# A decoder layer on one core: one map of SBUF for all passes, loads of the next pass ahead of its start, and the first maxima inside the query projection

## What is computed

```python
# block 1, per token: the half of the 2752 gated values that is smallest is set to 0
s = silu(x @ w_gate.T); s[smallest 1376 of abs(s)] = 0
x = layernorm(x + (s * (x @ w_up.T)) @ w_down.T)
# block 2: 32 query heads on 8 key/value heads of 32 columns
q = x @ Wq; k = ctx @ Wk; v = ctx @ Wv
x = layernorm(x + softmax(q k^T / sqrt(32)) v @ Wo)
# block 3: w dequantised from 4 bits to bf16
x = layernorm(x + (bf16(x) @ w.T))
```

## Time and profile before

| what | value |
|---|---|
| median of 3 runs | 2564.99 us (2564.35 to 2570.72) |
| profiled execution: its time, its span | 2554.46 us, 2552.7 us |
| mean granted TensorE clock | 0.975 |
| busy: TensorE, its weight loads | 2402.1 us (94%), 2089.8 us (82%) |
| busy: VectorE, ScalarE, GpSimd | 1249.4 us (49%), 1047.4 us (41%), 1421.9 us (56%) |

### The profile page before, as it was taken

The page is one execution under the profiler, slowest core; times in us unless marked ns, Lnnn a source line. Parts: engine busy times, 40 slices in busy tenths (PEclk is TensorE's granted clock), DMA queues, the critical chain, the costliest instruction groups (busy, mean ns, idle before and its releaser), DMA issues. The chain is left out here.

```text
span 2552.7 us, 32567 instructions
## 1 busy us (share of the span) xinstructions
PE 2402.1 (94%) x12627; PEld 2089.8 (82%) x12640; DVE 1249.4 (49%) x1770; ACT 1047.4 (41%) x1531; POOL 1421.9 (56%) x635
## 2 busy tenths in 40 slices
PE   7999799999999999999999999999978989885998
PEld 6999689988899888999889998899946666654775
DVE  4762201872016930058500386345258888863665
ACT  2112133733337333354423463233337777780211
POOL 5344154775546855459554486444429998891221
PEclk9999889999999999999999999999969999997999
DMA  6555432233322333223333233579767776646773
GB/s 205 170 191 177 144 125 101 103 122 124 114 99 108 122 103 134 99 99 108 121 125 114 91 108 106 176 239 295 219 158 185 189 184 167 172 108 170 177 175 95
DMA packets 245995, 371.70 MB, mean 146 GB/s; under 512 B 124336, under 2 KB 176560, under 8 KB 245584
## 3 DMA queue, kind: packets, MB, share of 16 engines
q1 hardware_dynamic: 245840, 369.60, 47.8%
HBM read 290.15 MB, written 78.70 MB: 144 GB/s over the span
## 5 line engine op out<-in xcount | busy, mean ns | idle before, releaser
L823 POOL TENSOR_TENSOR gp_w_lo<-gp_raw,gp_w_hi 128x1024 fp32r<-128x1024 f32 (+2 forms) x300 | 723.1, 2412 | 603.9 <-ACT gp_w_hi L707 603.4
L58 PE MATMUL gp_acc<-gp_x_hi,gp_w_hi 128*128 128x448 f32 x1504 | 560.7, 373 | 26.5 <-POOL gp_w_lo L823 19.6
L59 PE MATMUL gp_acc<-gp_x_lo,gp_w_hi 128*128 128x448 f32 x1504 | 551.0, 366 | 0.0
L60 PE MATMUL gp_acc<-gp_x_hi,gp_w_lo 128*128 128x448 f32 x1504 | 550.5, 366 | 0.0
L707 ACT CAST gp_w_hi<-gp_raw 128x1024 fp32r<-128x1024 f32 (+2 forms) x300 | 307.0, 1026 | 301.7 <-PE gp_acc L60 300.8
L1251 POOL TENSOR_TENSOR ap_e_lo<-ap_e,ap_e_hi 125x1344 fp32r<-125x1344 f32 x112 | 341.8, 3081 | 70.1 <-DVE ap_e_hi L1328 45.6
L58 PEld LDWEIGHTS gp_acc<-gp_x_hi,gp_w_hi 128*128 128x128 f32 x1504 | 283.8, 189 | 50.4 <-issue 19.7
L60 PEld LDWEIGHTS gp_acc<-gp_x_hi,gp_w_lo 128*128 128x128 f32 x1504 | 283.7, 189 | 23.1
L59 PEld LDWEIGHTS gp_acc<-gp_x_lo,gp_w_hi 128*128 128x128 f32 x1504 | 284.1, 189 | 20.8
L339 DVE TENSOR_REDUCE gp_sel_unit<-gp_keys 112x4 f32<-112x2048 f32 x4 | 9.2, 2289 | 567.0 <-ACT gp_keys L720 567.0
L58 PE MATMUL gp_acc<-gp_h_hi,gp_w_hi 128*128 128x448 f32 (+1 forms) x704 | 266.4, 378 | 7.8 <-DVE gp_h_lo L885 5.0
(11 more groups left out here) (163 smaller groups left out, 4288.7 us busy)
## 6 DMA issues: line engine op xcount, KB each, us to landing
gp_raw<-in_w_gu SPq DMA_DIRECT2D x172, 512.0 KB, 3.2
gp_raw<-in_w_d SPq DMA_DIRECT2D x80, 512.0 KB, 3.4
cp_c_raw<-in_ctx_t SPq DMA_DIRECT2D x32, 750.0 KB, 6.3
gp_raw<-in_w_q SPq DMA_DIRECT2D x32, 512.0 KB, 3.8
q_scratch<-gp_q_out SPq DMA_DIRECT2D x64, 224.0 KB, 5.5
ap_qs<-q_scratch SPq DMA_DIRECT2D x32, 448.0 KB, 4.9
o_scratch<-ap_o_ab SPq DMA_DIRECT2D x64, 224.0 KB
ap_vs<-v_scratch SPq DMA_DIRECT2D x16, 773.4 KB
```

Of the source, the lines that this page charges most:

```text
L58: nc.tensor.matmul(out, wh, xh, start=first, stop=False)
L59: nc.tensor.matmul(out, wh, xl, start=False, stop=False)
L60: return nc.tensor.matmul(out, wl, xh, start=False, stop=last)
L823: last = nc.gpsimd.tensor_tensor(o, i, hi.bitcast(F32), ALU.subtract)
```

## The change

All tensors get their address by hand. `Bufs` takes a starting place for each pass and counts upwards; class `Carry` holds what two passes share: the buffers of x and of the gated weights, the query and key tiles, the first value tile, the sums, and the first two output tiles, with their semaphores. On this map:

- context_pass loads the first four gated weight tiles and half of x of the first group when it has three batches to go. It ends without waiting for its stores; ScalarE and VectorE wait for them in the next pass, before they first write where stored tensors lay (`await_context`).
- In gated_query_pass VectorE instead of GpSimd makes the low parts of the first group's x. The loads for batch 0 and the first of batch 1 are issued between the query stores, and the 16 pairs of batch 0 with their maxima are put behind projections 23 to 29, the turn behind 30. The stores of the last queries are awaited by SyncE and ScalarE inside the attention pass.
- In attend_pass half 0 of the queries and keys two batches ahead is fetched at h = 3 instead of h = 4, which puts it ahead of a `put_o`. In the last batch SyncE loads the first two output tiles; VectorE makes their quotients at positions 17 and 20; tile 0 is also split there. One memset of ones is left at the start.
- In finish_pass the last reciprocals are made and stored beside the first projection, and the stores of the last batches are awaited ahead of tile 8.

```diff
     def sb(self, name, shape, dt):
-        return self.ctx.enter_context(self.nc.sbuf_tensor(f"{self.tag}_{name}", shape, dt))
+        at = self.place
+        self.place += (math.prod(shape[1:]) * self.SIZES[dt] + 31) // 32 * 32
+        if self.place > self.ROOM:
+            raise ValueError(name)
+        return self.nc.alloc_sbuf_tensor_at(f"{self.tag}_{name}", shape, dt, offset=self.BASE + at)
...
+class Carry:
...
+    IDENT, LOW, XW, ACTS, KEYS, EARLY, MASK, SMALL = 0, 768, 24320, 77568, 116992, 120576, 161024, 208768
+    C_STORED = 162816
+    Q_OUT = 106240
+    QK1 = 153280
+    WO, PARTS, E, FIN = 768, 66304, 179648, 153280
...
+    XR, RAW, NQO, NO = 2, 4, 4, 3
+    PUT = 2 * 16
...
+        m = Bufs(nc, ctx, "cy", self.LOW)
+        self.x_raw = [m.sb(f"x_raw{i}", [P, 2, T], F32) for i in range(self.XR)]
+        self.raw = [m.sb(f"raw{i}", [P, KD * P], F32) for i in range(self.RAW)]
+        m.jump(self.EARLY)
+        self.qs, self.ks = [None, None], [None, None]
+        self.qs[0] = m.sb("qs0", [3 * HD + 2, 2, REP, 4, S], F32R)
+        self.ks[0] = m.sb("ks0", [3 * HD + 2, 2, 4, CP], F32R)
+        self.vs0 = m.sb("vs0", [KN, KT, KV, VW], F32R)
...
+    def fetch_qk(self, sp, qd, kd, n, half):
+
+        p, stack = n % 2, 3 * HD
+        q_rows = self.qs[p][:, half].bitcast(F32).rearrange("d j m q -> d (j m q)")
+        k_rows = self.ks[p][:, half].bitcast(F32).rearrange("d v c -> d (v c)")
+        for dst, src in ((q_rows[0:2 * HD], qd[n, half]), (k_rows[0:HD], kd[n, half, 0:HD]),
+                         (q_rows[2 * HD:stack], qd[n, half, 0:HD]), (k_rows[HD:stack], kd[n, half])):
+            sp.dma_start(dst, src).then_inc(self.qk_loaded[p][half], 16)
+
+    def put_max(self, sp, n):
+        p, stack = n % 2, 3 * HD
+        sp.wait_ge(self.nml, n + 1)
+        for row, src in ((stack, self.nm_hi), (stack + 1, self.nm_lo)):
...
+def load_tile(sp, od, rd, i, num, add, rec, loaded):
+    t = slice(i * P, (i + 1) * P)
+    for n in range(i * P // S, ((i + 1) * P - 1) // S + 1):
+        q0, q1 = max(i * P - n * S, 0), min((i + 1) * P - n * S, S)
+        at = slice(n * S + q0 - i * P, n * S + q1 - i * P)
+        for s, dst in enumerate((num, add)):
+            sp.dma_start(dst[:, :, at], od[n, :, s].rearrange("h d j q -> (d j) h q")[:, :, q0:q1]).then_inc(loaded, 16)
+    for j in range(REP):
+        sp.dma_start(rec[j:P:REP], rd.rearrange("h j t -> j h t")[j, :, t].unsqueeze(0).broadcast_to([HD, KV, P])
+                     ).then_inc(loaded, 16)
 
...
                     for h in range(2):
                         load(n + 2, h)
                 store(n)
+                if n == B - 3:
+                    for i in range(cy.RAW):
+                        sp.dma_start(cy.raw[i][:], w_gu[i]).then_inc(cy.raw_loaded[i], 16)
+                        if i < cy.XR:
+                            sp.dma_start(cy.x_raw[i][:], x_t[0, :, 2 * i:2 * i + 2]).then_inc(cy.x_loaded[i], 16)
             sp.wait_ge(copied, KD)
-            sp.dma_start(w3_dram, w_io[:]).then_inc(w3_stored, 16)
-            for s in stored:
-                sp.wait_ge(s, 48 * (B // 2))
-            sp.wait_ge(w3_stored, 16)
+            sp.dma_start(w3_dram, w_io[:]).then_inc(cy.w3_stored, 16)
...
+    PAIRS = {23: (0, 1), 24: (2, 3), 25: (4, 5), 26: (6, 7), 27: (8, 9), 28: (10, 11, 12), 29: (13, 14, 15)}
+    TURN_MAX = 30
...
-            for i in range(XC):
+            for i in range(XR, XC):
                 load_x(0, i)
-                load(i)
-            for n in range(XC, NALL + AHEAD + 4):
+            for n in range(RAW, NALL + AHEAD + 4):
...
+                if p == 20:
+                    cy.await_context(sp)
+                    for s in q_stored:
+                        sp.wait_ge(s, 32 * KD // NQO)
+                    cy.fetch_qk(sp, q_v, k_v, 0, 0)
+                if p == 23:
+                    cy.fetch_qk(sp, q_v, k_v, 0, 1)
+                if p == 26:
+                    sp.dma_start(cy.vs0[:].bitcast(F32).rearrange("p t v w -> p (t v w)"), vd[0]).then_inc(cy.v_loaded[0], 16)
+                if p == 28:
+                    for i in range(XS):
+                        sp.wait_ge(y1_stored[i], 16 * len(range(i, B, XS)))
+                    sp.wait_ge(back, 2 * B)
+                    cy.fetch_qk(sp, q_v, k_v, 1, 0)
+                if p == 32:
+                    cy.put_max(sp, 0)
...
             for i in range(XC):
-                x_split_hi(0, i)
                 if i < SPL:
                     split_hi(i)
+                x_split_hi(0, i)
...
-            nc.gpsimd.memset(keep[:, :, I:], 0.0).then_inc(pads, 1)
-            pool.wait_ge(pads, 2)
-            for i in range(XC):
-                x_split_lo(0, i)
-                if i < SPL:
-                    split_lo(i)
+            for i in range(SPL):
+                split_lo(i)
...
+                if q == 1:
+                    pool.wait_ge(lo_done, N + q + SPL + 1)
+                    nc.gpsimd.memset(cy.ks[0][STACK:].bitcast(F32), 1.0).then_inc(cy.ones, 1)
+                    pool.wait_ge(cy.ones, 1)
...
+            def maxima(y):
+                hh, a = divmod(y, 2)
+                dve.wait_ge(cy.scored, y + 1)
+                nc.vector.reduce_max(cy.n_max[:, hh // 4, 2 * a:2 * a + 2, hh % 4], p_s[y % 2][:, :, 0:C],
+                                     AX_X).then_inc(cy.maxed, 1)
...
+            for i in range(XC):
+                k = slice(XK * i, XK * i + XK)
+                dve.wait_ge(x_hi_done, i + 1)
+                nc.vector.tensor_tensor(x_lo[:, k, :], x_raw[i % XR][:], x_hi[:, k, :].bitcast(F32),
+                                        ALU.subtract).then_inc(x_lo_done, 1)
+            cy.await_context(dve)
+            nc.vector.memset(keep[:, :, I:], 0.0)
...
+                for y in PAIRS.get(p, ()):
+                    maxima(y)
...
+            def first_pair(y):
+
+                hh, a = divmod(y, 2)
+                if y % (NPAIR // 2) == 0:
+                    pe.wait_ge(cy.qk_loaded[0][hh // 4], 64)
+                if y == 0:
+                    pe.wait_ge(added, B)
+                    pe.wait_ge(t_lo, 2 * B)
+                if y >= 2:
+                    pe.wait_ge(cy.maxed, y - 1)
+                for i in range(2):
+                    last = nc.tensor.matmul(p_s[y % 2][:, i, 0:CP], cy.qs[0][0:STACK, hh // 4, 2 * a + i, hh % 4, :],
+                                            cy.ks[0][0:STACK, hh // 4, hh % 4, :], start=True, stop=True)
+                last.then_inc(cy.scored, 1)
+
+            pe.wait_ge(pads, 1)
             for g in range(G):
                 for c in range(DOWN):
                     tile(g, c)
@@ -1056,6 +1237,12 @@
             for q in range(G * KD):
                 project(q)
                 between(q)
+                for y in PAIRS.get(q, ()):
+                    first_pair(y)
+                if q == TURN_MAX:
+                    pe.wait_ge(cy.maxed, NPAIR)
+                    nc.tensor.transpose(p_s[0][0:H, 0, 384:384 + S], cy.n_max[:].rearrange("q f j m -> q (f j m)"),
+                                        ident_f[0:S, 0:S]).then_inc(cy.nm_turned, 1)
...
                     if h == 0 and n + 1 < B:
                         fetch_qk(n + 1, 1)
-                    if h == KV // 2 and n + 2 < B:
-                        fetch_qk(n + 2, 0)
+                        if n == 0:
+                            cy.await_queries(sp)
                     if h == LAG and n + 1 < B:
                         fetch_v(n + 1)
+                    if h == KV // 2 - 1 and n + 2 < B:
+                        fetch_qk(n + 2, 0)
+                    if h == 2 and n == B - 1:
+                        sp.wait_ge(t_scored, NX * n)
+                        sp.wait_ge(r_stored, 16 * (B - GB))
+                        for i in range(2):
+                            load_tile(sp, od, rd, i, cy.num[i], cy.add[i], cy.rec[i], cy.o_loaded[i])
                     if (KV * n + h - LAG) % 2 == 0 and KV * n + h - LAG >= 2:
                         put_o((KV * n + h - LAG) // 2 - 1)
                     if h == RECIP_AT // KT and n % GB == 0 and n > 0:
...
-            put_recip(G - 1)
-            for i in range(NO):
-                sp.wait_ge(o_put[i], PUT * pairs_out(i, B))
-            sp.wait_ge(r_stored, 16 * B)
...
-            for p in range(2):
-                nc.gpsimd.memset(ks[p][STACK:KR].bitcast(F32), 1.0).then_inc(ones, 1)
+            nc.gpsimd.memset(ks[1][STACK:KR].bitcast(F32), 1.0).then_inc(ones, 1)
...
-            for y in range(NPAIR):
-                maxima(0, y)
-            max_lo(0)
...
+                    if n == B - 1 and x in QUOTIENTS_AT:
+                        quotients(QUOTIENTS_AT.index(x))
             follow(KV * B - 1)
-            invert(G - 1)
...
+                if i == LATE:
+                    for o in range(cy.NO):
+                        sp.wait_ge(cy.o_put[o], cy.PUT * cy.pairs_out(o, B))
+                    sp.wait_ge(cy.r_stored, 16 * B)
```

(8 more changed lines are left out.)

309 lines of the change are left out of this document (174 added, 135 removed).

## The result

| | before | after |
|---|---|---|
| median of the timed runs beside each other, us | 2564.99 (2561.78 to 2570.72) | 2554.84 (2551.80 to 2557.08) |
| profiled execution, us (span) | 2554.5 (2552.7) | 2557.1 (2555.3) |
| ratio after to before | | 0.9954, 95% interval 0.9942 to 0.9965 |

The kernel is faster, but by 10 us (0.5%) where 62 were forecast, and the time lies outside the range (2478 to 2530). Two differences have to be kept apart.

What follows compares the result with a forecast made beforehand. TensorE was busy 94% of the span, so only its idle time and slow stretches could be won. 14.5 + 20.0 + 14 + 13.5 = 62 us off the 2565 median gave 2503 us, range 2478 to 2530.

Steps and rivals of the forecast that it cites:

- First boundary: Context pass to gated pass: weights and half of x already loaded, no store awaited; gain 14.5 us, between 12 and 17.
- Second boundary: Last projection to first attention scores: 27.6 us of gap saved less 7.6 for pairs; gain 20.0 us, bounds 17.5 to 22.
- The pairs' part: Second boundary: 16 pairs put between the projections, with waits and transpose, cost 7.6 us; bounds 5.6 to 10.
- Inside attention: Key/query fetch ahead of the store of o shortens 13 waits by 1.1 us each; gain 14 us, bounds 0 to 26.
- fetch hidden anyway: Rival: value load, then maxima row, hold TensorE just as long; attention gains 2 us instead of 14; 2515 us, 20%.
- gains lost in some other way to about nothing: Rival for the whole kernel: the gains vanish in an unnamed way, leaving about the same time; 2%.
- addresses: Rival "Slower": TensorE reads operands at new addresses slower in the gated and query part; 2573 us, at 12 ns 2587; 4%.
- Third boundary: Attention to finish pass: two output tiles loaded in the last batch; gain 13.5 us, bounds 9 to 22.
- the chain: End of attention: splits and quotients on VectorE, each waiting for GpSimd, set the end; TensorE starts at 2311.3.
- The offset: Timed median lies 10.5 us above the profiled execution; the same difference taken for the changed kernel.
- At nothing: Map of addresses, PSUM order, and awaits placed where stores have long landed: counted as no gain or cost.

Runs made afterwards that it cites:

- e9: Changed kernel with the value load in two DMAs, the fetch behind the store of o, and the second quotient behind the last split: 2493.28 us.
- e3: Changed kernel, fetch left ahead of the store of o, each value load issued as two DMAs of 112 and 13 rows: 2502.95 us.
- e7: Kernel before with the value load in two DMAs of 112 and 13 rows and nothing else: 2542.51 us.
- e6: Changed kernel with the fetch back behind the store of o and the value load in two DMAs: 2496.15 us.
- e8: Changed kernel with the value load in two DMAs, and the second output tile's quotient moved behind the last split: 2493.82 us.
- e1: Changed kernel with one thing undone: the fetch two batches ahead back at h = 4, behind the store of o: 2520.65 us.

## Why the prediction was wrong, point by point

*First boundary, 14.5 forecast:* 14.9. The mechanism is right, the closeness is in part luck: the tile's end was put at 319.6 and came at 319.4, but by two errors of the same size. TensorE started 1.8 us later than said (310.26 against 308.5), since the context pass ended 1.7 later than in before's profile, and the waits inside the tile were 0.50 and 0.85 us, so that it took 9.1 us instead of 11.1.

*Second boundary, 20.0:* the gap gave 27.6, to the tenth as forecast. The pairs' part cost 8.3 (7.6 forecast): the last gated step on VectorE is 8.83 us ahead of before's (1603.29 against 1612.12), the last query step only 0.56. So 19.3. In the 8.3 lie 1.7 us of a stretch at half clock (next point); without it the pairs cost 6.6. The waits at the two groups of three were 0.69 and 0.70 us.

*Not in the sum:* between the first tile and 1603 the lead fell from 14.9 to 8.8, 6.1 us. The matmuls' mean is 367 ns where it was 366, but from one start to the next it is 203 ns in the median in both, so the addresses are not it. The clock record has three stretches of 3.4 us at half clock between the first tile and the last projection of after, two of them ahead of 1603 (from 598.8 and 936.7) and one behind (1674.0), each just after a wait of TensorE that before has with the same length (0.71, 0.71 and 0.62 us); before has no such stretch. The two are worth 3.4 us, the third the 1.7 named above. Of the rest of the 6.1, 0.6 is a slow start that lasts longer past the first tile, 0.6 are longer waits, and some 1.5 I can't place. In the other kernels with the new boundaries none (e9) to three (e3) such stretches fell, and from TensorE's first gated matmul to its last projection they took 4.3 to 10.6 us longer than before's profile, where the pairs less the shorter first tile are 4.1 (8.3 − 4.2). Why the clock falls there in one and not in the other stays open.

*Inside attention, 14:* this is the step that failed; it lost 43.6. Three errors lie in it. First, I let an earlier start mean an earlier end. The earlier trace rows showed the value load at the share of five engines, and I used it only to make the gain smaller, and wrote a lower bound of 0: a second load started into a running one takes rate from the one that has to finish first, and the bound had to go below nothing. Second, I costed the moved fetch and not what it was moved past. `put_o` carries the row of sums, VectorE waits for it in the reciprocal, and the low part of the maxima stands behind that on VectorE. The three batches where this happens lost 23.3 of the 43.6 us, 17.8 of it beyond what their neighbours lost. The earlier trace rows even showed the maxima row 0.69 late in such a batch. Third, I counted slow steps only as a gain, 2 us, when waits go; here, with waits of 3 us and more, the same matmuls took 18.5 us longer at a granted clock of 0.91. The rival nearest in kind, "fetch hidden anyway" at 2515, had the right doubt and the wrong sign. By the number the nearest was "gains lost in some other way to about nothing", to which I gave 2% and no mechanism. None of my rivals for the slow side was this one; the one I chose, addresses, is refuted by e7 and e6.

*Third boundary, 13.5:* 12.9. Here too two errors nearly cancel: the first quotient began 21.1 us after the last turn (22.8 forecast) and took 4.0 us instead of 2.5, with GpSimd beside it. The 13.5 are 2324.84 − 2311.3; the forecast's other wording, 24 less 8.5, gives 15.5, as it leaves out the low part of tile 0. e8 confirms the chain: one quotient out of the way is 2.7 us.

*The offset:* I added 10.5 us between profile and median for the changed kernel as for the old. Its median came 2.2 below its profile. Against its own profile the sum was off by 64.6 (2557.1 against 2492.5), against the median by 52; 57.6 are attention, 6.1 the gated pass, and the remaining terms add up to 1.

*At nothing:* the map of addresses is right (e6, e7), and TensorE's table of waits has none for the new awaits. With the failed line undone, e1 is 43.1 us below the kernel before by the medians, e6 against e7 46.4; the boundaries' 48 were nearly right.

## What to carry to other kernels

An earlier issue is not an earlier arrival: before a transfer is moved forward, look at what is in flight at that moment, on how many engines, and which of the two the program needs first. Of a moved issue, list what it now stands in front of, and follow each of those to its reader, and to what is queued behind that reader on its engine. And when a load shows at a third of the DMA share, mend that first: splitting 125 rows into 112 and 13 gave 23 us in the kernel before and 52 in the changed one, where the whole change had given 10.
